# A block's one-hots turned one block ahead, and one TensorE signal a block in place of three

## The chip, the cores and the metric

The kernel runs on one core of one Trainium2 chip. The metric is device time in microseconds (us) for one execution, and lower is better. TensorE is called PE here, VectorE DVE, ScalarE ACT, GpSimd POOL and SyncE SP, as the profile does.

## What is computed

A graph has 12,500 nodes with 64 features and 200,000 edges sorted by their destination `dst`. Three rounds of a message-passing layer (sums of neighbours' features by `src`, small matrix products, ELU) are added to x and normalised, and a second network, which sums edge features by `dst`, follows:

```python
neigh_mean = segment_sum(h[dst], src) * inv_deg
out = elu(h @ Wg + deg_pos * (neigh_mean @ Wl + h @ Ws) + b)          # three times
x = layernorm(x + out)
src_vec    = concat([x[node_i], stf]);      source_node_vec = segment_sum(src_vec, node_i) / cnt
target_vec = concat([x[node_j], ef, et]);   neighbors_sum = relu(segment_sum(target_vec @ W1.T + b1, node_i))
x = layernorm(x + concat([neighbors_sum, source_node_vec]) @ W2.T + b2)
```

## The kernel before

Edges are sorted into 544 blocks (`NB`) of 128 chunks; a chunk holds 4 edges (`K`), padded, and all edges of a block end in one tile of 128 nodes. The kernel goes through stages, one after the other: it ranks the edges, scatters them into a table in HBM, then makes a first pass over the blocks in the order of `dst` (`wide_by_dst`), a pass by `src` (`wide_by_src`), then spreads, sums and layers. This case is about `wide_by_dst`, which every engine has a function of that name for. The loops run over `NI` = 34 groups of 16 blocks (`TURN`); the first group stands outside of the hardware loop.

For block b the engines do the following in this stage. The short names in bold are used in the rest of the text.

- POOL gathers the block's rows from the table into `rows`, a ring of 8 slots (L613). It waits until block b-8 has left the slot.
- ACT **place(b+3)** copies the node numbers from the rows (L994) and waits for the gather to land.
- DVE **ones(b+2)** compares them with an iota (L1369). The result `oh` holds the 4 one-hot matrices of a block.
- PE **T(b)**, `turned`, transposes the one-hots (L747, 4 matmuls) into PSUM bank 2 or 3 and raises `tr`.
- ACT **oht(b)** copies them into SBUF (L1017). The trace calls the target `loc`, because the ring `oht` lies in the memory of `loc1`.
- ACT **whole(b+1)** makes the f32 copy `ohf` of the next block's one-hots (L1000).
- PE **F(b)**, `feature_sum`, multiplies them with the rows (L759, f32, 4 matmuls which the trace shows as 8) and raises `mm`.
- DVE **add(b)** adds that sum to the node table (L1415).
- DVE **hring(b)** copies the 192 values of the block's node tile out of the node table (L1406). Every 8 blocks, ahead of the first of them, DVE loads the 8 tile numbers into registers (`tiles`).
- PE **P(b)**, `pick`, multiplies the turned one-hots with hring (L752, 4 matmuls) and raises `gmm`.
- ACT (L1007) and DVE (L1396, L1397), both named **picked(b)**, copy the two halves of the result into `got`. SP writes `got` and `oht` to HBM, 4 blocks at a time.

Each engine runs its own list in order, and the engines meet at counting semaphores alone. The written order of PE is T(b), F(b), P(b). That of ACT is oht(b), picked(b-1), place(b+3), whole(b+1). That of DVE is hring(b), ones(b+2), picked(b-1), add(b).

Of the kernel before, what the change touches and what calls it, by code (L numbers as in the profile page):

```python
# [33 lines left out]
TURN = 16  # L34
# [36 lines left out]
def build(nc, x, src, dst, ef, stf, et, Wg1, Wl1, Ws1, b1, Wg2, Wl2, Ws2, b2, Wgo, Wlo, Wso, bo,  # L71
          W1t, c1, W2t, c2, out):
    with ExitStack() as ctx:
# [193 lines left out]
        class Wide:  # L267

            def __init__(self, name, k):
# [4 lines left out]
                self.tr = sem(f"{name}_tr")  # L274
# [3 lines left out]
                if k == 2:  # L278
                    self.row = sum_got
                    self.out = [sem(f"{name}_out{s}") for s in range(2)]  # L280
                    self.ohf = sem(f"{name}_ohf")
                    self.hc = sem(f"{name}_hc")
                    self.gmm = sem(f"{name}_gmm")
                    self.g = sem(f"{name}_g")
                    self.gv = sem(f"{name}_gv")
                    self.gout = [sem(f"{name}_gout{s}") for s in range(2)]
                else:
                    self.out = spread_out
                    self.got = sum_got[::4]
                    self.red = sem(f"{name}_red")  # L290

# [280 lines left out]
        def _(pool):  # L572
# [27 lines left out]
            def wide_by_dst(q):  # L600
                pool.wait_ge(s_hpad, 1)

                def body(i, first):
                    for c in range(TURN):
# [3 lines left out]
                        if not first or c > 7:  # L608
                            pool.wait_ge(q.mm, b - 7)
# [8 lines left out]
            def wide_by_src(q):  # L618
                pool.wait_ge(wide_d.mm, NB)
# [42 lines left out]
        def _(pe):  # L662
# [80 lines left out]
            def turned(q, b, u, bank, one_hots):  # L743
# [4 lines left out]
                mm.then_inc(q.tr, 1)  # L748
# [14 lines left out]
            def wide_by_dst(q):  # L763
                def body(i, first):
                    for c in range(TURN):
                        b, u = TURN * i + c, c % 2
                        pe.wait_ge(q.oh, b + 1)
                        if not first or c > 1:
                            pe.wait_ge(q.oht, b - 1)
                        turned(q, b, u, 2 + u, oh[:, c % 4])  # L770
# [3 lines left out]
                        feature_sum(u, ohf[:, u], rows[:, c % 8]).then_inc(q.mm, 1)  # L774
# [6 lines left out]
                        pick(4 + 2 * u, oht[:, c % 8, :], hring[:, c % 8, :]).then_inc(q.gmm, 1)  # L781
                loop(pe, body)
# [162 lines left out]
        def _(act):  # L945
# [45 lines left out]
            def wide_by_dst(q):  # L991
# [4 lines left out]
                def whole(b, c, first):  # L996
                    act.wait_ge(q.oh, b + 1)
                    if not first:
                        act.wait_ge(q.mm, b - 1)
                    act.copy(ohf[:, c % 2], oh[:, c % 4].rearrange("p n k -> p k n")).then_inc(q.ohf, 1)  # L1000

                def picked(b, c, first):

                    act.wait_ge(q.gmm, b + 1)
# [5 lines left out]
                def body(i, first, last=False):  # L1010
                    for c in range(TURN):
                        b, u = TURN * i + c, c % 2
                        act.wait_ge(q.tr, b + 1)
                        if c % 4 == 0 and not (first and c < 8):
# [3 lines left out]
                            q.oht, 1)  # L1018
                        if not first or c > 0:
# [3 lines left out]
                        if not (last and c == TURN - 1):  # L1023
                            whole(b + 1, c + 1, first and c < 1)
# [158 lines left out]
        def _(dve):  # L1183
# [202 lines left out]
            def wide_by_dst(q):  # L1386
# [4 lines left out]
                def picked(b, c, first):  # L1391

                    dve.wait_ge(q.gmm, b + 1)
# [6 lines left out]
                def body(i, first, last=False):  # L1400
                    for half in range(2):
                        at = tiles(2, TURN * i + 8 * half, 8, mybir.EngineType.DVE)
                        for e in range(8):
# [7 lines left out]
                            dve.wait_ge(q.mm, b + 1)  # L1411
# [294 lines left out]
```

## Time and profile before

| what | value |
|---|---|
| time, median of 3 runs | 10882.93 us (10874.25 to 10888.81) |
| the profiled execution | 10844.11 us, its span 10842.3 us |
| stage `wide_by_dst` in the span | 3232 to 4426 us |
| PE busy over the span | 65% |
| mean granted clock of TensorE | 0.874 |

The profiled execution is one execution of its own; its time lies 0.4% under the median of the three runs. Times in the rows are microseconds from the start of the span. A row of a timeline has the start, the duration, the engine, the line, the operation with out<-in, and the number of instructions merged; a bracket gives the idle time of the engine just before and what ended it. The ends of matmuls are modelled, their starts are not.

### The profile page before, as it was taken

The page shows a single profiled execution, that of the slowest core. Times are in us where ns is not written, and L with a number is a line of the kernel's source. Part 1 is how long each engine was busy: PE and PEld are TensorE (multiplying, and loading weights), DVE is VectorE, ACT ScalarE, POOL GpSimd, SP SyncE. Part 2 cuts the span into 40 slices and gives each one's busy share as a digit, 9 for nine tenths or more (in the row PEclk, how much of TensorE's full clock was granted, in tenths as well). Part 3 has the DMA queues.
Part 4 walks back from the last instruction along what each step waited for, and adds up shares of the span by engine and source line. Part 5 has one row for each costly group of instructions (what it writes and reads, how often), then busy time and mean ns, then how long its engine had stood idle before and what let it go on. Part 6 is the DMA issues. An engine that isn't in the chain of part 4 may idle for free.

```text
span 10842.3 us, 191817 instructions
## 1 busy us (share of the span) xinstructions
PE 7015.7 (65%) x46640; PEld 5921.0 (55%) x46640; DVE 6451.6 (60%) x15194; ACT 3571.9 (33%) x10119; POOL 5221.8 (48%) x4833
## 2 busy tenths in 40 slices
PE   7899981167009999655576665766645566666666
PEld 6688871167008888544444555445544455445556
DVE  8899980022016666544586556865567655675556
ACT  0133320000007777433394112931128511491111
POOL 0058886778654444566304662046620366306660
PEclk9999999999999999777698777987769877897776
DMA  9965555555559999665497665976648866896671
GB/s 385 389 192 143 146 143 139 142 127 126 133 137 308 305 304 301 202 168 166 90 376 269 197 198 111 377 251 195 198 83 338 287 197 197 243 392 193 196 188 28
DMA packets 1567388, 2320.61 MB, mean 214 GB/s; under 512 B 974516, under 2 KB 1046056, under 8 KB 1567320
## 3 DMA queue, kind: packets, MB, share of 16 engines
q1 hardware_dynamic: 1227608, 1356.73, 37.3%
q0 software_dynamic: 292608, 911.36, 30.7%
q10 hardware_dynamic: 47104, 51.75, 2.0%
q8 instruction: 26, 0.43, 0.0%
q14 instruction: 42, 0.34, 0.0%
HBM read 1328.55 MB, written 986.78 MB: 214 GB/s over the span
## 4 chain that ended last, share of the span: by engine, by line
issue 25%; PE 24%; another core or an unknown queue 16%; DVE 14%; ACT 8%; DMA 7%; DVEq 3%; POOL 2%; ACTq 2%; SPq 1%; POOLq 0%
PE ps L759 9%; PE ps L736 4%; DVE mask L1310 3%; ACT ring L1075 3%; PE ps L836 3%; ACT hring L1085 3%; DMA frows<-by_src 2%; PE ps L752 2%; DMA gathered<-ring 2%; DVE ohj L1228 2%; DVE prod L1294 2%; PE ps L747 1%; POOL ring L634 1%; PE ps L674 1%
## 5 line engine op out<-in xcount | busy, mean ns | idle before, releaser
L650 POOL DMA_INDIRECT ring<-gathered,gidx x2176 | 2190.3, 1007 | 3096.1 <-DMA gathered<-ring 1978.2
L580 POOL DMA_INDIRECT by_src<-prow,ppos x1562 | 1949.9, 1248 | 1225.6 <-DMA ppos<-pos 663.8
L836 PE MATMUL ps<-ring,oht_g 128*128 128x192 bf16 x8704 | 1169.5, 286 | 901.7 <-issue 651.0
L1383 DVE TENSOR_REDUCE red<-ps 128x256 f32<-128x768 f32 x680 | 649.9, 956 | 1515.6 <-remote 1010.3
L836 PEld LDWEIGHTS ps<-ring,oht_g 128*128 128x128 bf16 x8704 | 900.4, 124 | 1183.1 <-issue 1049.7
L1463 DVE CAST ring<-ps 128x384 bf16<-128x384 f32 x2176 | 1157.7, 555 | 311.5 <-PE ps L752 227.8
L752 PE MATMUL ps<-hring,oht_g 128*128 128x192 bf16 x8704 | 997.7, 248 | 514.2 <-ACT ring L1075 143.5
L1075 ACT CAST ring<-ps 128x384 bf16<-128x384 f32 x2176 | 1140.9, 527 | 10.9 <-PE ps L752 10.9
L752 PEld LDWEIGHTS ps<-hring,oht_g 128*128 128x128 fp8e4 x8704 | 658.8, 97 | 853.0 <-issue 830.9
L719 PE MATMUL ps<-snap,oht_e 98*128 98x98 f32 x3130 | 1056.8, 441 | 0.0
L1085 ACT COPY hring<-node 128x192 bf16 x2176 | 866.8, 399 | 76.3 <-issue 67.8
L759 PE MATMUL ps<-rows,ohf 128*128 128x193 f32 x4352 | 846.7, 338 | 26.3 <-ACT ohf L1000 20.3
L613 POOL DMA_INDIRECT rows<-by_src,gidx x544 | 517.5, 951 | 715.7 <-PE ps L759 271.3
L736 PE MATMUL ps<-steps,cmp 99*128 x2176 | 467.9, 352 | 562.0 <-issue 295.7
L719 PEld LDWEIGHTS ps<-snap,oht_e 98*128 98x128 f32 x3130 | 821.2, 323 | 0.0
L736 PEld LDWEIGHTS ps<-steps,cmp 99*128 99x128 f32 x2176 | 466.0, 333 | 564.2 <-issue 564.2
L973 ACT COPY snap<-ps 98x98 f32<-98x98 f32 x1565 | 376.7, 241 | 1186.0 <-PE ps L716 749.9
L759 PE MATMUL ps<-frows,oh_s 128*128 128x193 f32 x2176 | 567.2, 404 | 269.8 <-issue 162.9
L759 PEld LDWEIGHTS ps<-rows,ohf 128*128 128x128 f32 x4352 | 698.3, 190 | 43.5 <-ACT ohf L1000 31.9
L989 ACT COPY gidx<-move 128x4 int32 (+1 forms) x816 | 157.6, 197 | 1709.9 <-DVE node L1365 1627.5
L634 POOL DMA_INDIRECT ring<-gathered,gidx x544 | 562.3, 1034 | 324.4 <-issue 166.1
L1097 ACT CAST hring<-oh_s 128x512 f32<-128x512 bf16 x272 | 180.2, 662 | 1603.7 <-DVE oh_s L1369 801.0
(226 smaller groups left out, 12990.4 us busy)
## 6 DMA issues: line engine op xcount, KB each, us to landing
gathered<-ring SPq DMA_DIRECT2D x544, 768.0 KB
by_src<-zeros SPq DMA_DIRECT2D x34, 6272.0 KB, 45.9
frows<-by_src SPq DMA_DIRECT2D x544, 392.0 KB
oht_g<-oht SPq DMA_DIRECT2D x544, 256.0 KB, 4.8
gathered<-got SPq DMA_DIRECT2D x136, 776.0 KB
prow<-in_edge_attr_n SPq DMA_DIRECT2D x284, 352.0 KB
bc<-tidrow ACTq DMA_DIRECT2D x313, 160.0 KB
prow<-in_edge_attr SPq DMA_DIRECT2D x142, 352.0 KB
```

Source lines behind the costliest of these rows:

```text
L580: pool.indirect_dma_start(out=table, out_offset=bass.IndirectOffsetOnAxis(ap=ppos[:, s, j:j + 1], axis=0), in_=prow[:, s, j, :], in_offset ...
L634: pool.indirect_dma_start(out=ring1[:, c, :], out_offset=None, in_=gb1, in_offset=offsets(g, c % 4)).then_inc(q.got[g], 16)
L650: pool.indirect_dma_start(out=ring[:, c, :], out_offset=None, in_=gb, in_offset=offsets(g, c % 4)).then_inc(q.got[g], 16)
L719: pe.matmul(where, oht_e[0:T, v, l * P:(l + 1) * P], snap[0:T, (u * LANES + l) % 2, :], start=True, stop=False, skip_group_check=True).the ...
L736: mm = pe.matmul(flat[:, bass.ds(j * MV + (1024 * (k + 1) + c), 1)], cmp[0:T + 1, u, c, :], steps[k][0:T + 1, bass.ds(j * MV + c, 1)], sta ...
L752: mm = pe.matmul(ps[:, bank + k // 2, k % 2 * HW:(k % 2 + 1) * HW], eight(one_hots)[:, k * P:(k + 1) * P], parts, start=True, stop=True, s ...
L759: mm = pe.matmul(ps[:, bank, 0:FEAT], one_hots[:, k, :], rows_of[:, k, 0:FEAT], start=k == 0, stop=k == K - 1)
L836: mm = pe.matmul(ps[:, 2 * u + e // 2, e % 2 * 256:e % 2 * 256 + HW], ohq[:, c % 8, :, k], ring[:, c, k * HW:(k + 1) * HW], start=k == 0, ...
L1075: act.copy(ring[:, c, 0:2 * HW], ps[:, 2 * (c % 4), 0:2 * HW]).then_inc(q.g, 1)
L1085: act.copy(hring[:, e, :], parts_at(at[e])).then_inc(q.hc, 1)
L1383: return dve.tensor_reduce(red[:, u, :, 0:D], four_of(bank)[:, :, 0:HW].rearrange("p e (a d) -> p e d a", d=D), AX.X, ALU.add)
L1463: dve.tensor_copy(ring[:, c, 2 * HW:4 * HW], ps[:, 2 * (c % 4) + 1, 0:2 * HW]).then_inc(q.gv, 1)
```

## The change

PE no longer turns block b's one-hots at the start of block b. It turns those of block b+1 there, ahead of F(b) and P(b); block 0 is turned alone before the loop, and the last block turns nothing. The semaphores `tr` and `gmm` are gone in this stage (`tr` is left for the pass by `src`). One signal, `mm`, is raised by the last matmul of P(b), and everything that waited for T(b+1), F(b) or P(b) now waits for it. On ACT whole(b+1) moves up to stand right behind oht(b). The last group of 16 blocks is written out behind the hardware loop.

```diff
@@ class Wide
-                self.tr = sem(f"{name}_tr")
...
-                    self.gmm = sem(f"{name}_gmm")
...
+                    self.tr = sem(f"{name}_tr")
@@ POOL wide_by_dst
-                            pool.wait_ge(q.mm, b - 7)
+                            pool.wait_ge(q.mm, b - 6)
@@ PE
-            def turned(q, b, u, bank, one_hots):
+            def turned(bank, one_hots):
                 ...
-                mm.then_inc(q.tr, 1)
+                return mm
             def wide_by_dst(q):
-                def body(i, first):
+                def body(i, first, last=False):
                     for c in range(TURN):
                         b, u = TURN * i + c, c % 2
-                        pe.wait_ge(q.oh, b + 1)
-                        if not first or c > 1:
-                            pe.wait_ge(q.oht, b - 1)
-                        turned(q, b, u, 2 + u, oh[:, c % 4])
+                        if not (last and c == TURN - 1):
+                            pe.wait_ge(q.oh, b + 2)
+                            if not first or c > 0:
+                                pe.wait_ge(q.oht, b)
+                            turned(2 + (1 - u), oh[:, (c + 1) % 4])
                         pe.wait_ge(q.ohf, b + 1)
                         ...
-                        feature_sum(u, ohf[:, u], rows[:, c % 8]).then_inc(q.mm, 1)
+                        feature_sum(u, ohf[:, u], rows[:, c % 8])
                         ...
-                        pick(4 + 2 * u, oht[:, c % 8, :], hring[:, c % 8, :]).then_inc(q.gmm, 1)
-                loop(pe, body)
+                        pick(4 + 2 * u, oht[:, c % 8, :], hring[:, c % 8, :]).then_inc(q.mm, 1)
+                pe.wait_ge(q.oh, 1)
+                turned(2, oh[:, 0]).then_inc(q.mm, 1)
+                body(0, True)
+                with pe.Fori(1, NI - 1) as i:
+                    body(i, False)
+                body(NI - 1, False, True)
@@ ACT whole
-                        act.wait_ge(q.mm, b - 1)
+                        act.wait_ge(q.mm, b)
@@ ACT picked
-                    act.wait_ge(q.gmm, b + 1)
+                    act.wait_ge(q.mm, b + 2)
@@ ACT body, ahead of oht
-                        act.wait_ge(q.tr, b + 1)
+                        act.wait_ge(q.mm, b + 1)
                         ...
+                        if not (last and c == TURN - 1):
+                            whole(b + 1, c + 1, first and c < 1)
                         if not first or c > 0:
                             picked(b - 1, (c - 1) % TURN, first and c < 9)
                         if not (last and c > TURN - 4):
                             place(b + 3, c + 3)
-                        if not (last and c == TURN - 1):
-                            whole(b + 1, c + 1, first and c < 1)
@@ DVE picked
-                    dve.wait_ge(q.gmm, b + 1)
+                    dve.wait_ge(q.mm, b + 2)
@@ DVE body, ahead of add
-                            dve.wait_ge(q.mm, b + 1)
+                            dve.wait_ge(q.mm, b + 2)
```

On ACT, one block in the middle of the stage, with what each instruction waits for, stood before as follows (`loc1<-ps` is oht, `got` picked, `loc2` place, `ohf` whole; `sum_got11` is the landing of a gather, and `out0` that of an earlier write to HBM).

```order
L1017 CAST loc1<-ps 128x512 [waits wide_d_tr,wide_d_out0]
L1007 CAST got<-ps 128x2x192 [waits wide_d_gmm]
L994 CAST loc2<-rows 128x4 [waits sum_got11]
L1000 CAST ohf<-oh 128x512 [waits wide_d_mm,wide_d_oh]
L1017 CAST loc1<-ps 128x512 [waits wide_d_tr]
```

In the changed kernel the same place of ACT reads:

```order
L1024 CAST loc1<-ps 128x512 [waits wide_d_mm,wide_d_out0]
L1007 CAST ohf<-oh 128x512 [waits wide_d_mm,wide_d_oh]
L1014 CAST got<-ps 128x2x192 [waits wide_d_mm]
L1001 CAST loc2<-rows 128x4 [waits sum_got11]
L1024 CAST loc1<-ps 128x512 [waits wide_d_mm]
```

The copy `ohf` has moved from fourth to second place, and all the waits for PE are for one semaphore. Line numbers are shifted by 7.

On PE, the start of the stage (blocks 0 and 1) stood before as follows.

```order
L747 MATMUL ps<-ident_bf,oh 128x128 [waits wide_d_oh,s_ready]
L747 MATMUL ps<-ident_bf,oh 128x128 x3
L759 MATMUL ps<-rows,ohf 128x193 [waits wide_d_ohf]
L759 MATMUL ps<-rows,ohf 128x193 x3
L752 MATMUL ps<-hring,loc1 128x192 [waits wide_d_oht,wide_d_hc]
L752 MATMUL ps<-hring,loc1 128x192 x3
L747 MATMUL ps<-ident_bf,oh 128x128 [waits wide_d_oh]
```

In the changed kernel the start of the stage on PE reads:

```order
L746 MATMUL ps<-ident_bf,oh 128x128 [waits wide_d_oh,s_ready]
L746 MATMUL ps<-ident_bf,oh 128x128 x3
L746 MATMUL ps<-ident_bf,oh 128x128 [waits wide_d_oh]
L746 MATMUL ps<-ident_bf,oh 128x128 x3
L758 MATMUL ps<-rows,ohf 128x193 [waits wide_d_ohf]
L758 MATMUL ps<-rows,ohf 128x193 x3
L751 MATMUL ps<-hring,loc1 128x192 [waits wide_d_oht,wide_d_hc]
```

A second turning stands ahead of the first features; from there on PE goes through turning, features and picking in the same cycle as before, with a turning that is one block ahead.

## Rows read from the trace of the kernel before

**Rows 1.** The page's first line.

```profile
span 10842.3 us, 191817 instructions
```

**Rows 2.** The stage as one window; number of instructions in brackets.

```profile
core 0: us, PE busy (x) PEld busy (x) DVE busy (x) ACT busy (x) POOL busy (x), PEclk, DMA share, GB/s
3232.00:4426.00 1194.00, 1098.09 (x8704) 1019.67 (x8704) 748.54 (x2720) 889.36 (x2307) 513.88 (x541) 1.00 0.92 302
```

**Rows 3.** Timeline of PE, from block 5 of an eight to block 4 of the next.

```profile
3803.15 1.53 PE L759 MATMUL ps<-rows,ohf 128*128 128x193 f32 x8
3804.51 0.49 PE L752 MATMUL ps<-hring,loc 128*128 128x192 bf16 x4
3804.84 0.39 PE L747 MATMUL ps<-ident_bf,oh 128*128 128x128 bf16 x4
3805.08 1.57 PE L759 MATMUL ps<-rows,ohf 128*128 128x193 f32 x8
...
3808.98 1.57 PE L759 MATMUL ps<-rows,ohf 128*128 128x193 f32 x8
...
3810.68 0.49 PE L752 MATMUL ps<-hring,loc 128*128 128x192 bf16 x4
...
3811.22 1.53 PE L759 MATMUL ps<-rows,ohf 128*128 128x193 f32 x8
...
3813.16 1.57 PE L759 MATMUL ps<-rows,ohf 128*128 128x193 f32 x8
...
3814.90 0.39 PE L747 MATMUL ps<-ident_bf,oh 128*128 128x128 bf16 x4
...
3815.12 1.53 PE L759 MATMUL ps<-rows,ohf 128*128 128x193 f32 x8
...
3817.55 0.49 PE L752 MATMUL ps<-hring,loc 128*128 128x192 bf16 x4 [0.90 <-ACT loc L1017]
...
3818.50 1.57 PE L759 MATMUL ps<-rows,ohf 128*128 128x193 f32 x8 [0.24 <-ACT ohf L1000]
```

**Rows 4.** Timeline of DVE in the same stretch.

```profile
3804.82 0.36 DVE L1415 TENSOR_TENSOR node<-node,ps 128x193 f32 x1 [0.56 <-PE ps L759]
...
3808.72 0.36 DVE L1415 TENSOR_TENSOR node<-node,ps 128x193 f32 x1 [0.50 <-PE ps L759]
3810.36 0.21 DVE L1406 TENSOR_SCALAR hring<-node 128x192 bf16 x1 [1.29 <-issue]
...
3816.06 0.35 DVE L1415 TENSOR_TENSOR node<-node,ps 128x193 f32 x1 [1.81 <-PE ps L759]
```

**Rows 5.** Timeline of ACT in the same stretch.

```profile
3805.32 0.58 ACT L1017 CAST loc<-ps 128x512 fp8e4<-128x512 bf16 x1 [0.29 <-issue]
...
3806.27 0.67 ACT L1000 CAST ohf<-oh 128x512 f32<-128x512 bf16 x1
...
3816.82 0.58 ACT L1017 CAST loc<-ps 128x512 fp8e4<-128x512 bf16 x1 [1.81 <-PE ps L747]
```

**Rows 6.** Timeline of POOL in the same stretch.

```profile
3812.41 0.94 POOL L613 DMA_INDIRECT rows<-by_src,gidx  x1 [2.37 <-DVE got L1397]
...
3813.67 0.94 POOL L613 DMA_INDIRECT rows<-by_src,gidx  x1 [0.31 <-issue]
...
3815.11 0.94 POOL L613 DMA_INDIRECT rows<-by_src,gidx  x1 [0.50 <-issue]
```

**Rows 7.** Waits, 3300 to 4400 us: total us, times, longest us.

```profile
DVE node L1415 <- PE ps L759: 290.4, 321, 2.9
...
DVE hring L1406 <- issue: 79.0, 63, 1.6
PE ps L752 <- ACT loc L1017: 55.9, 64, 2.7
...
PE ps L759 <- ACT ohf L1000: 16.3, 60, 1.0
...
ACT loc L994 <- DMA rows<-by_src,gidx: 6.5, 12, 1.1
```

More of the change, by code:

```diff
@@ L618, in wide_by_src @@
             def wide_by_src(q):
-                pool.wait_ge(wide_d.mm, NB)
+                pool.wait_ge(wide_d.mm, NB + 1)
                 pool.wait_ge(wide_d.loc, NB)
```

## The prediction

> **What bounds the kernel now.** I read the page first: the span is 10842.3 us [rows 1], and the diff touches one stage of it. The window of that stage [rows 2] shows 8704 matmuls, 16 for each of 544 blocks, in 1194 us: 2.19 us a block. PE is busy for 1098.09 us of it, at a granted clock of 1.00 (the 2.4 GHz level), so PE is the engine to follow, and ACT (889.36 us) and DVE (748.54 us) have room. The timeline of PE [rows 3] says how much of PE's time is work. In an undisturbed stretch F starts at 3803.15 and, three blocks later, at 3808.98: 1.943 us a block, with P 1.36 us behind F, the next T 0.33 behind P, and the next F 0.24 behind T. PE waits for nothing there. 544 blocks at 1.943 us would be 1057 us, so about 137 us of the stage are stalls, some 5 of them at its start.
>
> The same rows show two stalls in every eight blocks. I number the blocks of an eight 0 to 7, block 0 being the one ahead of which DVE loads tile numbers.
>
> The **load stall**: F(0) starts at 3808.98 and F(1) at 3811.22, 2.24 us instead of 1.94, because P(0) starts only at 3810.68 instead of 3810.35. P(0) needs hring(0). DVE began add(7) at 3808.72, then sat 1.29 us on the register loads and began hring(0) at 3810.36 [rows 4]. These loads occur 63 times in 1100 us, 79.0 us in all [rows 7], and all but 0.3 us of each lies behind F(0).
>
> The **late-signal stall**: F(3) starts at 3815.12 and F(4) at 3818.50, 3.38 us instead of 1.94 [rows 3], a loss of 1.43. PE had started T(3) at 3814.90, but ACT began oht(3) only at 3816.82 [rows 5]. In the undisturbed stretch T starts at 3804.84 and oht at 3805.32, 0.48 later, so that the signal of T(3) is 1.44 us late. The signal of F(2) is late as well: DVE's add normally begins 1.67 us behind the start of F (3803.15 and 3804.82), here 3813.16 and 3816.06 [rows 3, 4], or 1.2 us late. PE itself went on: F(3) started 0.22 us behind T(3). So for some two microseconds PE computed while its signals did not arrive. What PE lost is 1.04 us on P(3) (3817.55, due at 3816.51), and then 0.4 us on F(4), since whole(4) stands last on ACT (P to F 0.95 us instead of 0.57). Ahead of these stretches POOL issued three gathers at 3812.41, 3813.67 and 3815.11 [rows 6], 2.7 us for three where the undisturbed pace needs 3.9: DVE had been held by the loads and then caught up. PE waited for ACT in this way 64 times for oht and 60 times for ohf in 1100 us [rows 7], about once in each eight blocks. 68 eights at 0.3 and 64 at 1.43 make 112 us of the 137; the rest is scattered.
>
> **The change part by part.** PE's matmuls are the same in number and cyclic order. One T moves ahead of F(0) of the stage: 0.3 us, once. The last group outside of the loop issues the same instructions. So the undisturbed 1.943 us stand. I cost the three moved waits one after the other.
>
> *T(b+1) ahead of F(b)* needs ones(b+1) a block earlier. DVE does ones(b+1) within block b-1, behind hring(b-1), that is about 1 us behind the signal of P(b-2) (add 0.36, hring 0.21, ones 0.42), and PE wants it 1.94 us behind that signal: hidden, with 0.9 us of cover. Behind a load DVE needs 1.3 more, but PE then stands on hring(0) too, and ones(2) is done some 0.35 us behind the end of hring(0), where T(2) is due 0.4 us behind it: nothing, with little cover.
>
> *oht(b) waits for P(b-1) instead of T(b).* P(b) is due 1.45 us behind the arrival of the signal of P(b-1) (1.94 less about 0.5 from the start of P to the arrival). ACT needs 0.7 of it (0.58 and its latencies) [rows 5], which leaves 0.75 us. whole(b+1), now behind oht, is ready at 1.3 us where F(b+1) is due at 2.0. picked(b-1) and place(b+3) end at about 1.8, before the next signal. So ACT hides this, and the 0.4 us on F(4) are gone: 64 × 0.4 = 26 us saved.
>
> *add(b) waits for P(b) instead of F(b)*: DVE starts 0.33 us later, in each block. DVE has 0.56 us of idle time before add [rows 4], and that does not shrink, as its whole list slides. But the load of tile numbers stands behind add(7), so hring(0) slides 0.33 us against PE, and there nothing covers it: the load stall grows from 0.33 to 0.66 us. 68 × 0.33 = 22 us lost. The gathers, which wait for picked on DVE, slide by 0.33 us too; ACT waited only 6.5 us in 1100 for a landing [rows 7], so I cost this at nothing.
>
> *One signal in place of three* decides the sum. Let L be the lateness of the signal of P that falls into the disturbed stretch. P(b+1) then stalls for L − 0.75 us. The trace has no single signal of this sort; the nearest rows are the first held one, F(2), late by 1.2 us, and T(3), late by 1.44, as third in the row. Bounds are 0 (the signal of P(2) falls outside: P(0) slides from 3810.68 to 3811.01, so P(2) starts at 3814.9 and signals 0.5 us later, at 3815.4, and P(3) at 3817.35, while the third gather slides to between 3815.4 and 3815.7; in the rows signals were held from 3814.8 at the latest to 3816.8, from 0.3 us before the third gather to 1.7 behind it) and 2.9 us, the longest wait of add for PE [rows 7]. I take 1.2, as one signal would be the first held. The stall is then 0.45 us instead of 1.04, or 0.45 instead of 1.43 with the 0.4 above.
>
> By rule of the Trainium skill ("TensorE: Matmul & The Clock Gate", The cost: per-tile semaphore tail), completion increments of matmuls serialise at 26.3 ns each; two fewer in each of 544 blocks would be 29 us as an estimate, were they on the path. The trace does not agree that they are: in the undisturbed stretch PE never waits for its own signals. The skill's "Perfetto Trace Analysis" (Tensor Engine Instruction) adds that a matmul's end in a profile is an estimate and that its signal leaves when PSUM has acknowledged; the late starts of DVE and ACT agree, with 1.2 and 1.44 us.
>
> **Sum.** For each eight +0.33 (load) and 0.45 − 1.43 = −0.98 (late signal), together −0.65 us; times 64: −42 us. On the profiled execution that is 10844.1 − 42 = 10802 us. The median of the runs shown, 10882.93 us, lies 38.8 us above it, and the forecast is made for such a median: 10882.9 − 41.9 = **10841 us**. A difference of 0.2% (22 us) is about what a measurement of this kernel tells from none.
>
> **The rivals**, as values of L, with 64 × (0.33 + L − 0.75 − 1.43).
>
> *The signal is held to the end of the stretch, so the stall only moves.* L between 1.5 and 2.2 us gives −22 to +22 us: 10861 to 10905, no change. For it: ACT's and DVE's waits end within a few tenths of 3816.8 whichever signal they wait for. Against it: F(2)'s signal came half a microsecond or more before T(3)'s. Chance 0.26.
>
> *Slower: with one signal all three consumers hang on the one that is held.* From L = 2.2 us on the change loses, since DVE's add, ACT's oht and the gathers then start together, and the load stall's 22 us stay unpaid. L = 2.4 gives +35 us, 10918. For it speaks the longest wait of 2.9 us; against it that the stretch in which signals were held was about 2 us, so that this needs one that starts just before P(2) ends, every time. Chance 0.16.
>
> *The stretch passes between two signals, or does not arise.* With one signal in 1.94 us instead of three, and gathers 1.35 to 1.6 us apart instead of 1.26 and 1.44, no signal need be late: L under 0.75, −70 us, 10812. A floor under this is the DMA engines, busy for a share of 0.92 at 2.19 us a block [rows 2]; at 2.02 us a block they would be full, −95 us. Chance 0.20.
>
> **How the numbers follow.** My case (L from 0.75 to 1.5, −22 to −70 us) has 0.38. The range takes in the DMA floor on one side (10788) and the whole of the no-change case on the other (10905); the slower case, 0.16, is left out: 10786 to 10905. Faster by over 0.2%: 0.36 of my case, all 0.20 of the third, 0.01 of the first, 0.57. Slower: 0.13 of the slower case and 0.03 of the first, 0.16. The same: 0.27.
>
> **What would show it.** In the profile after: undisturbed F to F stays at 1.94 us; F(0) to F(1) grows from 2.24 to about 2.57; DVE's add starts 2.0 us behind F instead of 1.67; PE's waits for ACT ohf are gone; F(3) to F(4), or the blocks around it, falls from 3.38 to about 2.4; the window of the stage is some 42 us shorter, the other stages unchanged. I am wrong if the load stall grows by more than a third of a microsecond, since T(2) has almost no cover there; if DVE, now released later, sets the pace in plain blocks; if other signals than the one I follow become late; or if the gathers, issued later, are waited for by place.

## The result and the profile after

The changed kernel takes 10792.21 us (median of 4 runs, 10779.35 to 10799.14) where the kernel before takes 10885.87 us beside it (4 runs, 10874.25 to 10904.9): a ratio of 0.9908, with a 95% interval of 0.9891 to 0.9924. That is 94 us less. The forecast was faster by 42 us with a range that holds 10792, so the sign and the range held, and the size was less than half of what came.

The time comes out of the stage. The changed kernel's stage as one window, to set against [rows 2], and the row of F from the view of its tile, whose last two times are the starts of the first and the last matmul:

```profile
3229.00:4337.00 1108.00, 1067.31 (x8704) 1005.51 (x8704) 754.38 (x2720) 902.66 (x2307) 521.90 (x541) 0.99 0.96 326
```

```profile
L758 PE MATMUL ps<-rows,ohf x4352: 327/327/688, 3232.7 to 4334.8; 128*128 128x193 f32 x198
```

The window is 1108 us instead of 1194, with the same instructions. From the first F to the last it is 1102.1 us (4334.8 − 3232.7); the same row of the kernel before reads 3235.4 to 4424.0, 1188.6 us. I call this stretch, from the start of the first F to that of the last, **the stage's length** below; it is 86.5 us shorter here. The profiled execution as a whole takes 10779.35 us. What follows the stage is 6416 us in the profile of before (10842.3 − 4426) and 6440 here (10777.5 − 4337), with the same code, so that the two profiled spans differ by only 64.8 us; the profiled execution of before lies 42 us under the median of its kernel, the changed kernel's 13 us under its own. So I read the stage and not the span. The profiles of the runs b2, c3, d1 and d2 below are of executions that were 1 to 2.4% longer overall than the medians beside them, outside of this stage, and only the stage is read from them.

The timeline of PE in the changed kernel, from block 7 of an eight to block 4 of the next, answers to [rows 3]; T is left out of the rows:

```profile
3812.07 1.53 PE L758 MATMUL ps<-rows,ohf 128*128 128x193 f32 x8
...
3813.99 1.53 PE L758 MATMUL ps<-rows,ohf 128*128 128x193 f32 x8
...
3815.83 0.49 PE L751 MATMUL ps<-hring,loc 128*128 128x192 bf16 x4 [0.32 <-issue]
...
3816.49 1.53 PE L758 MATMUL ps<-rows,ohf 128*128 128x193 f32 x8
3817.85 0.49 PE L751 MATMUL ps<-hring,loc 128*128 128x192 bf16 x4
...
3818.40 1.53 PE L758 MATMUL ps<-rows,ohf 128*128 128x193 f32 x8
3819.76 0.49 PE L751 MATMUL ps<-hring,loc 128*128 128x192 bf16 x4
...
3820.32 1.53 PE L758 MATMUL ps<-rows,ohf 128*128 128x193 f32 x8
...
3822.23 1.53 PE L758 MATMUL ps<-rows,ohf 128*128 128x193 f32 x8
```

Three things differ. F(3) to F(4) is 1.91 us (3820.32, 3822.23), where it was 3.38: the late-signal stall is gone. F(0) to F(1) is 2.50 us, where it was 2.24: the load stall has grown. And the plain pace is 1.916 us instead of 1.943. Summed over the starts of all F in the trace, the gaps F(3) to F(4) hold 76 us above 1.92 us each in the kernel before and 1 us in the changed one, the gaps F(0) to F(1) 29 and 40 us, and all the other gaps 40 and 17 us. The 76 us stand in 52 eights of the 68, with a gap of over 3 us; in the other 16 it is the plain one.

DVE, ACT and POOL around the same eight, to set against [rows 4 to 6]:

```profile
3814.07 0.36 DVE L1422 TENSOR_TENSOR node<-node,ps 128x193 f32 x1 [0.50 <-PE ps L751]
3815.52 0.21 DVE L1413 TENSOR_SCALAR hring<-node 128x192 bf16 x1 [1.09 <-issue]
...
3820.64 0.36 DVE L1422 TENSOR_TENSOR node<-node,ps 128x193 f32 x1 [0.80 <-PE ps L751]
```

```profile
3818.43 0.58 ACT L1024 CAST loc<-ps 128x512 fp8e4<-128x512 bf16 x1 [0.40 <-issue]
...
3820.59 0.59 ACT L1024 CAST loc<-ps 128x512 fp8e4<-128x512 bf16 x1 [0.52 <-PE ps L751]
```

```profile
3817.58 0.94 POOL L612 DMA_INDIRECT rows<-by_src,gidx  x1 [2.20 <-DVE got L1404]
3818.84 0.95 POOL L612 DMA_INDIRECT rows<-by_src,gidx  x1 [0.31 <-issue]
3820.70 0.94 POOL L612 DMA_INDIRECT rows<-by_src,gidx  x1 [0.92 <-PE ps L751]
```

P(1) starts at 3817.85 and oht(2) 0.58 us later; P(2) starts at 3819.76 and oht(3) 0.83 us later, at 3820.59. The signal of P(2) is still late, but by 0.25 us, which PE does not feel. The gathers come 1.26 and 1.86 us apart, 3.12 us for the three, where they took 2.70. PE's waits in this stage, against [rows 7]:

```profile
DVE hring L1413 <- issue: 60.3, 62, 1.5
...
ACT loc L1001 <- DMA rows<-by_src,gidx: 45.7, 72, 2.0
...
PE ps L751 <- ACT loc L1024: 12.9, 13, 2.7
```

PE waits for oht 13 times in 1000 us instead of 64 in 1100. ACT now waits for gathers to land, 45.7 us where it was 6.5.

### The profile page after: what moved, and what is told of

The parts are those of the page before. It is cut to its first block and busy times, and to the rows that moved or that the text cites. A ratio compares the mean times of both kernels' runs of the same rounds, so it can differ in the third digit from the quotient of the medians.

```text
span 10777.5 us, 191831 instructions
## 1 busy us (share of the span) xinstructions
PE 6987.1 (65%) x46640; PEld 5926.1 (55%) x46640; DVE 6446.5 (60%) x15194; ACT 3586.6 (33%) x10119; POOL 5204.1 (48%) x4833
## 5 line engine op out<-in xcount | busy, mean ns | idle before, releaser
L1390 DVE TENSOR_REDUCE red<-ps 128x256 f32<-128x768 f32 x680 | 650.2, 956 | 1565.4 <-remote 1172.7
L1082 ACT CAST ring<-ps 128x384 bf16<-128x384 f32 x2176 | 1132.1, 521 | 12.8 <-PE ps L751 12.8
L1337 DVE TENSOR_TENSOR cmp<-iota_row,thr 99x1024 f32<-99x1024 f32 x136 | 166.4, 1226 | 1337.0 <-remote 929.3
```

The costliest lines, as they stand in the source:

```text
L1082: act.copy(ring[:, c, 0:2 * HW], ps[:, 2 * (c % 4), 0:2 * HW]).then_inc(q.g, 1)
L1390: return dve.tensor_reduce(red[:, u, :, 0:D], four_of(bank)[:, :, 0:HW].rearrange("p e (a d) -> p e d a", d=D), AX.X, ALU.add)
```

## The experiments

The late-signal stall is where most of the 86.5 us came from, so the question is what made it go. My theory after the result is **BURST**: signals are held up when POOL issues three gathers close together, and the change spreads them, since add, and with it DVE's catching up, waits for P. Its first rival is **COUNT**: signals are held because there are three a block. A second, **MERGED**, has the merged wait itself keep the stall away. **COVER** is the part that turning ahead may play: a late signal has more time before PE needs what hangs on it.

The trace of the kernel before already speaks for BURST. By the starts of its gathers and of F, in 52 of the 66 eights between the first and the last POOL starts three gathers within 2.9 us around P(2), and each of the 52 has the stall; of the other 14 none has it.

Each run is compared with the kernel before, run beside it on the same chip. "Length" is the stage's length defined above. Gaps are medians over the 68 eights, from the starts of F in the trace. A ratio needs both kernels in several executions, so c3, d1 and d2, with one execution each, have none.

| run | from | ratio (95%) | length, us | F(3) to F(4) | F(0) to F(1) |
|---|---|---|---|---|---|
| before | | | 1188.6 | 3.38 | 2.25 |
| changed | | 0.9908 (0.9891 to 0.9924) | 1102.1 | 1.92 | 2.42 |
| a1 idle signals | changed | 0.9876 (0.9769 to 0.9983) | 1102.4 | 1.92 | 2.40 |
| a2 add after pick | before | 0.9982 (0.9948 to 1.0016) | 1195.2 | 2.76 | 2.46 |
| a3 gathers paced | before | 0.9939 (0.9897 to 0.9980) | 1132.1 | 1.97 | 2.22 |
| a4 whole second | before | 0.9953 (0.9905 to 1.0001) | 1159.8 | 3.12 | 2.26 |
| b1 three signals | changed | 0.9936 (0.9916 to 0.9957) | 1115.0 | 2.06 | 1.95 |
| b2 add on features | changed | 0.9957 (0.9943 to 0.9971) | 1144.8 | 2.90 | 2.31 |
| b3 order and pace | before | 0.9907 (0.9884 to 0.9930) | 1092.0 | 1.92 | 2.31 |
| b4 whole last | changed | 0.9943 (0.9918 to 0.9967) | 1143.1 | 1.92 | 2.53 |
| c1 b2, paced | changed | 0.9961 (0.9946 to 0.9975) | 1081.7 | 1.92 | 2.16 |
| c2 b1, paced | changed | 0.9937 (0.9919 to 0.9955) | 1069.4 | 1.92 | 2.04 |
| c3 quarter write | before | one execution | 1082.4 | 1.93 | 2.27 |
| c4 changed again | changed | 0.9963 (0.9952 to 0.9974) | 1088.1 | 1.92 | 2.37 |
| d1 before again | before | one execution | 1189.6 | 3.38 | 2.25 |
| d2 quarter write again | before | one execution | 1178.6 | 3.37 | 2.36 |
| d3 changed again | changed | 0.9940 (0.9907 to 0.9972) | 1100.0 | 1.92 | 2.35 |
| d4 b1, paced, again | changed | 0.9889 (0.9864 to 0.9914) | 1069.9 | 1.92 | 2.04 |

Runs with the same letter ran on the same chip, and each letter is another chip. The kernel before took 10896.88 us (median) beside the runs a, 10839.46 beside b, 10355.42 beside c and 10845.49 beside d. The times expected for the runs b were stated for a kernel before at 10886 us; beside them it took 46 us less, so lengths and gaps decide there. Lengths of different letters are compared below across chips; that of the kernel before was 1188.6 us where it was first profiled and 1189.6 us on the chip of the runs d.

**a1, two idle signals in the changed kernel.**

```diff
-                            turned(2 + (1 - u), oh[:, (c + 1) % 4])
+                            turned(2 + (1 - u), oh[:, (c + 1) % 4]).then_inc(q.idle_t, 1)
...
-                        feature_sum(u, ohf[:, u], rows[:, c % 8])
+                        feature_sum(u, ohf[:, u], rows[:, c % 8]).then_inc(q.idle_f, 1)
```

> The changed kernel with two more signals a block, raised by the last matmul of T(b+1) and of F(b) on semaphores that nothing waits for. Theory BURST (TensorE's signals are held up after three gathers in under about 2.7 us, and the change breaks such bursts up because add, and with it DVE's catching up, waits for P): the same as the changed kernel, 10785 to 10805 us, F(3) to F(4) stays at 1.92. Theory COUNT (signals get held because there are three of them a block): the late-signal stall comes back at least in part, 10830 to 10880 us.

The length is 1102.4 us, 0.3 us from the changed kernel. Two more signals a block cost nothing, and bring no stall back: COUNT has fallen. The idle signals show something more: the trace's record of increments has that of F(2) late by 0.5 us (median), while that of P(2) is late by 0.25. Signals are still held up at this place, for a shorter time, and P(2), the one that the changed kernel waits for, comes near the end of the hold.

**a2, add waits for P, in the kernel before.**

```diff
-                            dve.wait_ge(q.mm, b + 1)
+                            dve.wait_ge(q.gmm, b + 1)
```

> The kernel before with one wait changed: DVE's add(b) waits for the signal of P(b) instead of that of F(b). All three signals, the order of PE and that of ACT stay. BURST: gathers behind a load spread out as in the changed kernel and the late-signal stall (74 us in the profile) goes, the load stall grows by 10 to 22 us, together 10815 to 10845 us. COUNT: the late signals stay and only the load stall grows, 10890 to 10910 us.

The time, 10895.24 us, is the one that COUNT gave, but the trace does not show the signals as late as before. The gathers did spread (1.26 and 1.76 us apart), and the holds got shorter (F(2) 0.57, P(2) 0.31, T(3) 0.83 us late against 1.2, 1.6 and 1.4). But T(3) is what oht(3) waits for here, and 0.83 us is more than its cover: F(3) to F(4) is 2.76. The load stall grew by 0.2 us. Together the length is 1195.2, 6.6 us longer. Spreading the gathers a little is not enough while oht hangs on T(b). BURST had the direction of the holds right and, in taking them to vanish, the time wrong.

**a3, gathers paced, in the kernel before.** One wait of POOL is made stricter by one block of F:

```diff
-                            pool.wait_ge(q.mm, b - 7)
+                            pool.wait_ge(q.mm, b - 6)
```

> The kernel before, with POOL's gather for block b+8 waiting for F(b+1) instead of F(b) (which comes some 0.4 us before the gather in plain blocks, so that only bursts are spread). BURST: the third gather of a burst comes 0.4 to 0.5 us later (spacing 1.25 and 1.9 instead of 1.25 and 1.44), most of the late-signal stall goes, 10810 to 10850 us. COUNT: no change, 10875 to 10895 us.

The gathers behind a load are 1.27 and 2.39 us apart (medians), F(3) to F(4) falls to 1.97, and the length by 56.5 us. PE's order, ACT's order and all three signals are those of before. Starting the third gather later takes the late-signal stall away by itself.

**a4, whole second on ACT, in the kernel before.**

```diff
+                        if not (last and c == TURN - 1):
+                            whole(b + 1, c + 1, first and c < 1)
                         if not first or c > 0:
                             picked(b - 1, (c - 1) % TURN, first and c < 9)
                         if not (last and c > TURN - 4):
                             place(b + 3, c + 3)
-                        if not (last and c == TURN - 1):
-                            whole(b + 1, c + 1, first and c < 1)
```

> The kernel before with whole(b+1) moved on ACT to stand right behind oht(b), as in the change, and nothing else. By the prediction's own term it saves the 0.4 us on F(4) behind a late signal, 20 to 26 us: 10860 to 10866 us, with F(3) to F(4) at 3.0 instead of 3.4. If the prediction's term is wrong, 10880 to 10890.

28.8 us of the length, and not where I had put them. F(3) to F(4) falls by 0.26 us, some 14 us in all. The rest is the pace: every gap between plain blocks is 1.916 us, where the kernel before has 1.964 and 1.934 in turn. In the kernel before F(b) starts 0.73 us behind the start of whole(b) in every second block (0.77 and more in the others), and whole takes 0.67 us [rows 5]; with whole second it is 1.18 us. So PE did wait for `ohf`, by a few hundredths of a microsecond in plain blocks. No row shows that as idle time; the modelled ends of matmuls can cover it. The ratio alone would not tell this run from the kernel before, as its interval reaches 1.0001; the length and the gaps do.

**b1, the changed kernel with three signals, each for its own consumers.**

```diff
+                            turned(...).then_inc(q.ts, 1)
+                        feature_sum(...).then_inc(q.fs, 1)
...
-                        act.wait_ge(q.mm, b + 1)
+                        act.wait_ge(q.ts, b + 1)
...
-                            dve.wait_ge(q.mm, b + 2)
+                            dve.wait_ge(q.fs, b + 1)
-                            pool.wait_ge(q.mm, b - 6)
+                            pool.wait_ge(q.fs, b - 7)
```

> The changed kernel (T(b+1) ahead of F(b), whole second on ACT) with three signals a block, each waited for by its own consumers as in the kernel before: oht by T, add, whole and the gathers by F, picked by P. BURST, with the theory that turning ahead gives COVER: DVE catches up behind a load as before, gathers come 1.26 and 1.44 apart, the signals of F(2), P(2), T(4) are held by 1.2 to 1.6 us again, but T's signal has 2.6 us of cover now and nothing stalls; the load stall goes back by some 11 us: 10770 to 10795 us. If only the one late signal keeps the stall away (MERGED), the late-signal stall returns: 10830 to 10860.

The length is 1115.0, between the two. The holds are back (P(2) late by 1.56, T(4) by 1.36 us), and turning ahead covers most of them: F(3) to F(4) 2.06, 17 us in all instead of 76. DVE and POOL now bunch a second time in each eight, which costs 23 us at block 6. The load stall is almost gone (1.95): add is not slid (1.67 us behind F), and hring(0) follows add(7) by 1.22 us (medians), where it was 1.64. Why DVE's loads take less time there, no run shows.

**b2, the changed kernel with a signal of its own for add.**

```diff
-                        feature_sum(u, ohf[:, u], rows[:, c % 8])
+                        feature_sum(u, ohf[:, u], rows[:, c % 8]).then_inc(q.fs, 1)
...
-                            dve.wait_ge(q.mm, b + 2)
+                            dve.wait_ge(q.fs, b + 1)
```

> The changed kernel with a signal of its own for F(b), on which only DVE's add waits; all else waits for P. BURST: the gathers behind a load are 1.26 and 1.44 us apart again, the signal of P(2) is held by about 1.6 us, oht(3) hangs on it and P(3) stalls for 1.6 less 0.75: about 50 us more in the stage and 11 less at the loads, 10820 to 10840 us. If the spacing of the gathers is not the cause, only the load stall shrinks: 10775 to 10790 us.

This is the reverse test, and the late-signal stall comes back. Timelines of POOL, PE and ACT in b2, blocks 2 to 4 of an eight:

```profile
3921.61 0.95 POOL L613 DMA_INDIRECT rows<-by_src,gidx  x1 [2.26 <-DVE got L1405]
3922.87 0.95 POOL L613 DMA_INDIRECT rows<-by_src,gidx  x1 [0.31 <-issue]
3924.40 0.95 POOL L613 DMA_INDIRECT rows<-by_src,gidx  x1 [0.58 <-ACT loc L1002]
```

```profile
3923.79 0.49 PE L752 MATMUL ps<-hring,loc 128*128 128x192 bf16 x4
3924.35 1.53 PE L759 MATMUL ps<-rows,ohf 128*128 128x193 f32 x8
3926.71 0.49 PE L752 MATMUL ps<-hring,loc 128*128 128x192 bf16 x4 [0.83 <-ACT loc L1025]
3927.26 1.53 PE L759 MATMUL ps<-rows,ohf 128*128 128x193 f32 x8
```

```profile
3925.98 0.59 ACT L1025 CAST loc<-ps 128x512 fp8e4<-128x512 bf16 x1 [1.90 <-remote]
```

Three gathers in 2.79 us; P(2) starts at 3923.79 and oht(3) only 2.19 us later instead of 0.58, so that the signal is 1.6 us late; P(3), due at 3925.71, starts at 3926.71. F(3) to F(4) is 2.91 here. The stage is 42.7 us longer than the changed kernel's, with 49 us more in these gaps (about 50 expected) and 9 us less in the load stall. With L = 1.6 the formula of the prediction, L − 0.75, gives 0.85 us for P(3); the median is 0.98.

**b3, the kernel before with the edits of a3 and a4 together.**

> The kernel before with both single edits that helped: whole(b+1) second on ACT, and the gather for block b+8 waiting for F(b+1). T is not ahead and all three signals stay. BURST: the gains of the two add up but for the 0.4 us on F(4), which both remove: the stage's F(0) to F(543) at 1110 to 1120 us (1187 before, 1101 in the changed kernel), time 10800 to 10825 us. If turning ahead or the merged signal is needed for most of the gain: 10840 to 10870.

Length 1092.0, which is 96.6 less than before and 10 less than the changed kernel; the gains of a3 (56.5) and a4 (28.8) add up, with 11 more that neither has alone (in a3 plain blocks still run at 1.93 to 1.97 us, here at 1.916). I had expected 1110 to 1120 us, so this is 18 us better than my range. T is not ahead and three signals are kept: neither is needed for the gain, and MERGED has fallen with it.

**b4, the changed kernel with whole last on ACT** (the edit of a4 in reverse).

> The changed kernel with ACT's list as it was before, whole(b+1) last. If the pace of the plain blocks (1.943 us before, 1.916 in the changed kernel) comes from ohf, which on every other block was finished only 0.05 us ahead of F, it goes back to 1.94: 544 x 0.027 = 15 us more, 10800 to 10815 us. If the pace comes from PE's order: no change, 10785 to 10800.

The pace stays at 1.916 in most plain blocks, against my expectation: the signal of P(b-1), for which oht(b) waits now, comes some 0.2 us ahead of that of T(b) in the kernel before (oht starts 0.59 us behind P(b-1) instead of 0.81), so that whole, even as last, is ready 0.2 us earlier than before. Yet the stage is 41.0 us longer than the changed kernel's. The waits of ACT and PE in b4's stage:

```profile
ACT loc L1001 <- DMA rows<-by_src,gidx: 75.9, 91, 2.1
...
PEld ps L758 <- ACT ohf L1007: 52.5, 77, 1.8
...
PE ps L758 <- ACT ohf L1007: 40.8, 70, 1.6
```

In the changed kernel's stage the last two rows hold 1.0 and 0.8 us. ACT's place(b+3) waits for gathers to land there too (75.9 us here, 56.5 in the changed kernel), and with whole behind place PE waits along. Of the changed kernel's 86.5 us, 41 hang on this one line of ACT.

**c1 and c2, b2 and b1 with paced gathers; c3, the kernel before with a quarter of the write of `got`; c4, the changed kernel again.** The edit of c1 against b2 (c2 against b1 is the same from `q.fs, b - 7`), and that of c3:

```diff
-                            pool.wait_ge(q.mm, b - 6)
+                            pool.wait_ge(q.fs, b - 6)
```

```diff
-                        sp.dma_start(blocks(gb1_v, 4 * j, 4, G1W), together(got[:, 4 * h:4 * h + 4, :])).then_inc(
+                        sp.dma_start(blocks(gb1_v, 4 * j, 1, G1W), together(got[:, 4 * h:4 * h + 1, :])).then_inc(
```

> The changed kernel with a signal of its own for F, on which add waits, and the gather for block b+8 waiting for F(b+1). BURST: the spread gathers take the late-signal stall away again (49.8 us in block 3's gap without them), and the load stall is the small one of the kernel before: F(0) to F(543) at about 1090 us, 8 to 12 us faster than the changed kernel in the same call. If the late signals come from DVE's earlier add and not from the gathers, 1140 us and slower than the changed kernel by 30 to 40.

> T(b+1) ahead, three signals a block with their own consumers, whole second, and the gather for block b+8 waiting for F(b+1). BURST and COVER: no signal is late by more than 0.6 us and oht has the most cover of all variants, the load stall falls below that of the kernel before (hring is the only thing left): F(0) to F(543) at 1070 to 1090 us, the fastest of the call. If bursts arise elsewhere in this variant (its first run had a second one in each eight), 1095 to 1115.

> The kernel before, with SP writing only one in four of a group's blocks of got to HBM in this stage; the rest of that array is zeros, written at the start, so that the output is not the reference's, and only the stage wide_by_dst is to be read. If the held signals come from the gathers alone (BURST), the gap F(3) to F(4) stays at about 3.4 us and the stage at 1180 to 1190. If the write of got to HBM, which runs between the gathers, is needed for it, the gap falls to about 1.95 and the stage to 1110 to 1130.

> The changed kernel as it is, for comparison on the same chip: ratio to the kernel before 0.991 as measured, between 0.989 and 0.993, whatever the theory, and F(0) to F(543) at 1101 us.

c3 alone would have read as: the write to HBM makes the holds. But c4 had gained only 0.37% on this chip, not the 0.7 to 1.1% that I had expected whatever the theory, and in the record of increments of all four traces none of PE's signals in this stage is late. Over the whole execution 16 or 17 of them are late by 0.5 to 1.8 us in each of the four, where it is 644 in the kernel before. The timelines of POOL, PE and ACT in c3:

```profile
3770.18 0.95 POOL L616 DMA_INDIRECT rows<-by_src,gidx  x1 [2.50 <-DVE got L1400]
3771.43 0.95 POOL L616 DMA_INDIRECT rows<-by_src,gidx  x1 [0.31 <-issue]
3772.88 0.95 POOL L616 DMA_INDIRECT rows<-by_src,gidx  x1 [0.50 <-PE ps L762]
```

```profile
3772.68 0.39 PE L750 MATMUL ps<-ident_bf,oh 128*128 128x128 bf16 x4
```

```profile
3773.15 0.59 ACT L1020 CAST loc<-ps 128x512 fp8e4<-128x512 bf16 x1 [0.37 <-PE ps L750]
```

The three gathers are as close as in [rows 6] (2.70 us), and oht(3) starts 0.47 us behind T(3), on time. Three gathers within 2.9 us stand in 50 of c3's eights, and none has the stall. So the chip matters, or something that goes with it. c1 (1081.7) and c2 (1069.4) are 6.4 and 18.7 us shorter than the changed kernel (1088.1) on it; c1, meant to show that paced gathers take the stall away again, can't show it where none arises.

On this chip the stage does not account for the gain. The kernel before was not profiled there. By c3's length, and 11 us for the three quarters of the write (d1 against d2 below), an estimate for it is 1093 us, 5 more than the changed kernel's; the median times differ by 44 us. Where the other 39 us come from, no run shows.

**d1 to d4, all on one more chip.**

> The kernel before, unchanged, profiled in the same call as the next two. If held signals are a matter of the chip as well, its gap F(3) to F(4) may be near 1.95 instead of 3.38, and its stage near 1120 instead of 1187 us. If not, 3.4 and 1180 to 1190, and the ratio of the changed kernel is 0.991 again.

> The kernel before with one in four of the blocks of got written to HBM in the stage (output not the reference's), now beside the kernel before on one chip. GATHERS ALONE: same gap F(3) to F(4) as the kernel before in this call. WRITE NEEDED: 1.95 where the kernel before has 3.4.

> The changed kernel beside the kernel before, both profiled on one chip. If the kernel before shows the late-signal stall in this call: ratio 0.990 to 0.993. If it shows none: 0.996 to 0.997, the gain of the pace alone (15 us) and of the waits for ohf, less the longer load stall.

> T ahead, three signals, gathers spread, on the same chip: 15 to 30 us faster than the changed kernel whether or not held signals occur on this chip, since its load stall is shorter by 0.33 us or more and its gathers are never bunched.

d1 repeats the stage of before to 1 us. d2 settles the write. Its timelines of POOL, PE and ACT:

```profile
3935.45 0.94 POOL L616 DMA_INDIRECT rows<-by_src,gidx  x1 [2.50 <-DVE got L1400]
3936.70 0.94 POOL L616 DMA_INDIRECT rows<-by_src,gidx  x1 [0.31 <-issue]
3938.15 0.95 POOL L616 DMA_INDIRECT rows<-by_src,gidx  x1 [0.50 <-issue]
```

```profile
3937.93 0.39 PE L750 MATMUL ps<-ident_bf,oh 128*128 128x128 bf16 x4
```

```profile
3939.84 0.58 ACT L1020 CAST loc<-ps 128x512 fp8e4<-128x512 bf16 x1 [1.78 <-PE ps L750]
```

oht(3) starts 1.91 us behind T(3), with a quarter of the write: F(3) to F(4) is 3.37, where d1 has 3.38. Three quarters of the write of `got` are not needed for the holds; the length falls by 11 us elsewhere. d3 repeats the changed kernel's stage to 2 us; its ratio, 0.9940, lies just above the 0.990 to 0.993 expected, which its interval takes in. d4 (T ahead, three signals, gathers paced, whole second) is 30.1 us shorter in the stage than d3 and, at 10725.97 us against 10753.95, the fastest of the runs d, with a ratio to the kernel before of 0.9889 (0.9864 to 0.9914). No run compared it with b3 on one chip. The gaps F(0) to F(1) are 2.04 us, close to the plain pace: oht, whole and hring all have cover.

## Why the prediction was right and wrong

The direction was right, and so was the reading of the two stalls and of the gain from ACT's order. The step that failed is **"One signal in place of three decides the sum"**. It took the hold on TensorE's signals as given (L = 1.2 us) and asked only which signal would fall into it, so that a stall of 0.45 us was left. The runs show that the number of signals does not matter (a1: 0.3 us, and b3 keeps all three) and that the hold itself shrinks with the spacing of the gathers: P(2) is late by 0.25 us instead of 1.6, and nothing of the stall is left. The spacing was the term that the prediction put at nothing: it let the gathers slide by 0.33 us as a whole and looked only at the wait of place for them.

The gaps between the starts of F add up to the stage's length, so each term of the sum can be set against what it measured:

| gaps | predicted, us | measured, us |
|---|---|---|
| F(3) to F(4), the late-signal stall | 64 × (0.45 − 1.43) = −63 | −75 |
| F(0) to F(1), the load stall | 64 × 0.33 = +21 | +11 |
| all others | 0 | −23 |
| sum | −42 | −86.5 |

- **The late-signal stall** holds two errors of opposite sign. The rest of 0.45 us in each of 64 eights, 29 us, did not come. But the stall before was also counted too high, at 64 × 1.43 = 92 us: the 64 waits of PE for oht [rows 7] were read as one stalled gap each, and only 52 gaps were stalled, 76 us in all.
- **"PE waits for nothing there"** (the undisturbed 1.943 us stand) was wrong. whole was ready only just ahead of F, and a4 showed 1.916 us for plain blocks once it moved: 544 × 0.027 = 15 us that I had not counted, about half of the −23 in the other gaps and a little of the −75. I had written that whole stands last on ACT and had seen its cost only behind a late signal. The row to compare was whole's end (3806.94, 6.27 + 0.67) with F(7)'s start at 3807.05.
- **The load stall** was taken to grow by 0.33 us, and grew by about half of that. hring(0) follows add(7) by 1.45 us in the eight shown (3814.07, 3815.52), 1.33 in the median, instead of 1.64, so that part of the slide is absorbed in the loads. The little cover that I named for T(2) was indeed too little in that eight: from P(0) to F(1) are 0.66 us (3815.83, 3816.49) instead of 0.55.

I had given a rival of 0.20 to no signal being late, with gathers further apart among its reasons, and it came nearest (−70 us, with −95 as the floor). The range held 10792 because it was drawn down to the floor of that rival, not because my own case was near: that the time came inside is in part luck.

Of the rest: the 0.33 us by which add slides is in the rows (2.00 us behind F instead of 1.67). The order of ACT, which I priced at 26 us behind late signals, gave 28.8 us alone in the kernel before and 41 us in the changed one, though half of the 28.8 is pace and not the late signals. I had said that the landing of gathers would not be waited for; ACT does wait, 45.7 us in 1000, and only with whole ahead of place does it cost next to nothing. The price of completion increments did not show: two more a block changed the length by 0.3 us, so they are not on the path. The rule of the Trainium skill ("TensorE: Matmul & The Clock Gate", The cost: per-tile semaphore tail) would make them 29 us as an estimate; the trace does not agree that this adds to the stage. The floor from the DMA engines did not hold as a bound: d4 runs the stage at 1.97 us a block, under the 2.02 at which I had them full.

What is shown: on the chips of the runs a, b and d, the late-signal stall goes when only the gathers are spread (a3), returns when the changed kernel lets them bunch (b2), and does not depend on the number of signals (a1) or on three quarters of the write of `got` (d2). A merged wait is neither needed for that (b3) nor enough (b2, where oht waits for P as in the changed kernel). Turning ahead helps by the cover it gives to oht: with the holds back, b1 has 17 us in the gaps F(3) to F(4), where the kernel before has 76.

Open is by what path bunched gathers hold up TensorE's signals, and what differs on the chip of the c runs. One rival stands untested: that the holds come with the recording of the profile. Every execution on record carries a granted clock, so none shows the kernel unrecorded. And the records of increments are incomplete on the chips that show holds: of the 544 increments of F, P and T in the stage, the trace of the kernel before has 499, 518 and 403, and of the 544 of ACT's `got` 291, while c1, c2 and c4 have them all but one or two, and c3 those of F, P and `got`, with 504 of T. The held signals are real in these executions, as DVE and ACT start late by them; whether they are there without the recording, no run shows.

## What to carry to other kernels

When an engine is seen to go on while its consumers start late, compare the start of the consumer with the start of the producer's last instruction in plain and in disturbed stretches; the difference is the lateness of the signal, and what happened on the queues of gathers just ahead is the place to look. A producer that catches up after a pause and then issues its gathers back to back can cost more than the pause did: one stricter wait, satisfied in plain blocks anyway, was worth 56 us here on a chip that shows held signals, and together with one moved line it gave at least what the whole change gave (96.6 us of the stage against 86.5). In an in-order engine, put the copy that TensorE waits for ahead of instructions that wait for DMA, and compare ends with starts before calling a pace undisturbed: a wait of some hundredths of a microsecond in every block has no row of its own.

## What the runs showed of the hardware

In recorded executions TensorE's signals can arrive 1.2 to 1.6 us late (F(2), T(3) and P(2) of the kernel before) while the matmuls go on, with three indirect gathers issued within 2.7 to 2.8 us on GpSimd; with 3.1 us for the three, P(2) was 0.25 us late. The "Perfetto Trace Analysis" page of the Trainium skill (Tensor Engine Instruction) has the signal leave on PSUM's acknowledgement, behind an estimated end; the trace agrees that the end is no measure of the signal, with 1.6 us between them. That an acknowledgement is what is late, no run here shows. In one eight of the kernel before the increments of P(2), T(3) and F(3), which stand for a whole block of work, are recorded within 0.2 us, at 3799.36, 3799.42 and 3799.51, when the hold ends.

One of the chips showed no hold in this stage and hardly a late signal in the others, and ran both kernels 4 to 5% faster. The sums further on show the difference in the group of their reduction, first in the changed kernel's profile and then in c4, the same kernel on that chip:

```profile
L1390 DVE TENSOR_REDUCE red<-ps 128x256 f32<-128x768 f32 x680 | 650.2, 956 | 1565.4 <-remote 1172.7
```

```profile
L1390 DVE TENSOR_REDUCE red<-ps 128x256 f32<-128x768 f32 x680 | 650.2, 956 | 1036.4 <-PE ps L843 829.3
```

DVE sits idle for 1565.4 us ahead of it on the one and 1036.4 on the other, 529 us less, where the spans differ by 481.5 (10777.5 and 10296.0). Where the releaser is "remote" on the one, one that the profile can't name, it is PE on the other. That these waits are held signals is likely but not shown. A gain that comes from such holds may differ from chip to chip: the changed kernel gained 0.9% where it was first measured (ratio 0.9891 to 0.9924) and 0.4% beside the runs c (0.9952 to 0.9974). The 0.6% beside the runs d (0.9907 to 0.9972) can't be told from either.

The granted clock of the changed kernel's first 1600 us is 0.51 (the level of 1.2 GHz) where the kernel before has 1.00 (2.4 GHz), and PE's busy time there is the same, 1438.82 and 1438.84 us for the same 7884 matmuls within that stretch. The granted clock of a profile was no measure of PE's speed in that stretch.
